# Reordering the first stage of a perceiver block: loads, first key products and two groups of queries

## The reference

```python
x = x + xattn(layernorm(x), context)   # 16 heads of 64; this is the layer that the change touches
x = x + gla(layernorm(x))              # gated linear attention, 4 heads
x = x + moe(layernorm(x))              # 8 experts, top 2, then layernorm

# xattn
q = tanh(x @ Wq);  k, v = split(context @ Wkv)
k = tanh(concat(null_key, k));  v = concat(null_value, v)
out = softmax(q k^T / 8) @ v           # over 1024 keys and the null key
return out @ Wout + bout
```

## Time and profile before

| | us |
|---|---|
| median of 3 runs | 219.04 (218.93 to 219.86) |
| profiled execution | 215.93 |
| its span, first to last instruction | 214.1 |
| TensorE busy | 194.7 (91%) |
| VectorE busy | 147.1 (69%) |
| ScalarE busy | 119.2 (56%) |
| GpSimd busy | 39.2 (18%) |
| mean granted TensorE clock | 0.992 |

### The profile page before, as it was taken

How to read it: one execution, slowest core, us unless ns; L and a number is a source line. 1 busy time by engine, 2 the same in 40 slices (tenths; PEclk the granted TensorE clock), 3 DMA queues, 4 the chain that set the end, 5 groups by cost and what they waited for, 6 DMA issues and landing times.

```text
span 214.1 us, 4143 instructions
## 1 busy us (share of the span) xinstructions
PE 194.7 (91%) x1621; PEld 146.2 (68%) x1621; DVE 147.1 (69%) x265; ACT 119.2 (56%) x218; POOL 39.2 (18%) x40
## 2 busy tenths in 40 slices
PE   6794879799999999999999999969888899999992
PEld 1692778688889898878889877946565334635560
DVE  3459798689888899998888869833892747134303
ACT  3197588588888888887888864102612113231300
POOL 4139202204022031220220800020501400000001
PEclk9999699999999999999999999999999999999999
DMA  5896559971103011010000596899999500000000
GB/s 170 283 388 171 134 164 369 367 205 54 49 3 98 3 49 52 0 49 3 0 5 0 193 384 211 288 385 378 377 377 377 175 0 0 3 0 0 5 0 26
DMA packets 22853, 31.02 MB, mean 145 GB/s; under 512 B 1953, under 2 KB 18866, under 8 KB 22834
## 3 DMA queue, kind: packets, MB, share of 16 engines
q1 hardware_dynamic: 22834, 30.76, 43.0%
HBM read 29.57 MB, written 0.13 MB: 139 GB/s over the span
## 4 chain that ended last, share of the span: by engine, by line
PE 45%; issue 22%; DVE 11%; DMA 8%; SPq 5%; ACT 5%; POOL 3%; POOLq 0%; DVEq 0%
PE ps L1001 30%; PE ps L1035 5%; DMA stage_t<-in_ctxT 4%; DMA w_k_stage<-in_Wkv 3%; SPq L433 3%; DVE keys L723 3%; PE ps L1075 2%; PE ps L1089 2%; DVE qx L835 1%; ACT keys L569 1%; DVE mixT L733 1%; POOL ctxT_l L477 1%; DVE att L862 1%; SPq L426 1%; PE ps L1152 1%
## 5 line engine op out<-in xcount | busy, mean ns | idle before, releaser
L723 DVE SCALAR_TENSOR_TENSOR keys<-ps,keys 64x512 f16<-64x512 f32 x64 | 44.1, 689 | 7.1 <-ACT keys L569 5.7
L1001 PE MATMUL ps<-ctxT_h,w_k_h 128*128 128x256 f32 x128 | 39.7, 310 | 3.1 <-POOL ctxT_l L477 1.6
L569 ACT ACTIVATE keys<-ps 64x512 f16<-64x512 f32 x64 | 37.8, 591 | 1.8
L1001 PE MATMUL ps<-ctxT_l,w_k_h 128*128 128x256 f32 x128 | 36.9, 288 | 0.0
L1001 PE MATMUL ps<-ctxT_h,w_k_l 128*128 128x256 f32 x128 | 36.7, 287 | 0.0
L1001 PEld LDWEIGHTS ps<-ctxT_h,w_k_h 128*128 128x128 f32 x128 | 25.0, 195 | 4.8 <-issue 2.4
L565 ACT ACTIVATE ps<-ps 128x512 f32<-128x512 f32 x32 | 18.6, 582 | 16.1 <-PE ps L1001 16.1
L689 DVE TENSOR_TENSOR ex_l<-ps,ex_h 128x512 fp32r<-128x512 f32 x32 | 22.1, 691 | 7.0 <-ACT ps L599 6.5
L1001 PE MATMUL ps<-ex_h,ctx_h 128*128 128x512 f32 x64 | 25.7, 401 | 0.0
L1001 PE MATMUL ps<-ex_l,ctx_h 128*128 128x512 f32 x64 | 25.3, 395 | 0.0
L1001 PEld LDWEIGHTS ps<-ctxT_l,w_k_h 128*128 128x128 f32 x128 | 25.2, 197 | 0.0
(11 more groups left out here) (173 smaller groups left out, 258.0 us busy)
## 6 DMA issues: line engine op xcount, KB each, us to landing
w<-in_fc1T SPq DMA_DIRECT2D x8, 1024.0 KB, 12.3
w<-in_fc SPq DMA_DIRECT2D x8, 1024.0 KB, 11.9
stage_t<-in_ctxT SPq DMA_DIRECT2D x8, 256.0 KB, 4.7
stage_n<-in_ctx SPq DMA_DIRECT2D x8, 256.0 KB, 4.1
w_k_stage<-in_Wkv SPq DMA_DIRECT2D x4, 256.0 KB, 5.4
mixT<-in_Wq SPq DMA_DIRECT2D x2, 512.0 KB, 6.3
q_two<-q_split SPq DMA_DIRECT2D x8, 128.0 KB, 4.4
w_v<-in_Wkv SPq DMA_DIRECT2D x1, 1024.0 KB, 5.3
```

The costliest lines, as they stand in the source:

```text
L569: nc.scalar.activation(keys[rows, u % 2, PK * i:PK * (i + 1), r], full[rows].rearrange("p (j n) -> p j n", j=PK), ACT.Copy, scale=UNIT).th ...
L723: V.scalar_tensor_tensor(out=keys[other, u % 2, PK * i:PK * (i + 1), r], in0=ps[mine, K_BANK + kp % 2].rearrange("p (j n) -> p j n", j=PK) ...
L1001: last = MM(dst, lhs[i], rhs[j], start=start and m == 0, stop=stop and m == len(parts) - 1)
```

## The change

SP's list is reordered: ctxT 0 first, then x, Wk 1, the identity, and the queries' weights and the rest of Wk by turns; the copies of the queries come ahead of the constants and the small loads. Wk 0 is loaded by ScalarE's own queue. TensorE makes key products 0 and 1 part by part as their operands become ready (`first_keys`), with the transposes in between, then the queries in two groups with keys 2 and 3 between and behind them; product 3 is done ahead of step 0 instead of in it. ScalarE and VectorE follow: VectorE makes the high part of context piece 0 and of Wk 2 and 3. GpSimd's memset of the sums moves to its beginning. In the steps one line changes: the high part of ctxT n+2 is made in step 4n + 1 instead of 4n + 3, in all pieces. The warm-up goes from 8 and 2 products to 7.

```diff
@@ SP
+            load_ctxT(0)
             sp.dma_start(x0[:], a["x"]).then_inc(ld_x, 16)
+            load_wk(1)
             sp.dma_start(const[:, 0:C_STRICT], a["const"][:, 0:C_STRICT]).then_inc(ld_eye, 16)
-            load_wk(0)
-            load_ctxT(0)
...
-            load_wk(1)
+            load_wq(0)
+            load_wk(2)
+            load_wq(1)
+            load_wk(3)
             sp.dma_start(null_k[:], a["null_k"]).then_inc(ld_null, 16)
             sp.dma_start(null_v[:], a["null_v"]).then_inc(ld_null_v, 16)
-            load_wk(2)
-            load_wk(3)
             load_ctx(0)
             load_ctxT(1)
             load_ctx(1)
...
+            spread_queries(0)
+            spread_queries(1)
             sp.dma_start(const[:, C_STRICT:], a["const"][:, C_STRICT:]).then_inc(ld_const, 16)
...
             sp.dma_start(b1[:], a["b1"]).then_inc(ld_small, 16)
...
-            spread_queries(0)
-            spread_queries(1)
@@ GpSimd
             nc.gpsimd.memset(minus_half[:], -0.5).then_inc(half_ready, 1)
+            nc.gpsimd.memset(ex_sum[:], 0.0).then_inc(zero_ready, 1)
...
-                    nc.gpsimd.memset(ex_sum[:], 0.0).then_inc(zero_ready, 1)
@@ ScalarE
+            act.dma_start(w_k_piece(w_k_stage, 0), w_k_source(0)).then_inc(ld_wk[0], 16)
             split_wk(0)
-            act.wait_ge(ld_ctxT[0], 16)
-            copy(ctxT_h[:, 0], stage_t[:, 0], first_high)
             split_wk(1)
+            keys_tanh(0)
+            keys_tanh(1)
+            queries_tanh(0)
             act.wait_ge(ld_null, 16)
             nc.scalar.activation(null_kt[:], null_k[:], ACT.Tanh).then_inc(nk_tanh, 1)
...
             keys_tanh(2)
+            queries_tanh(1)
+            null_exp(0)
+            keys_tanh(3)
@@ VectorE
+            dve.wait_ge(ld_ctxT[0], 16)
+            V.tensor_copy(ctxT_h[:, 0], stage_t[:, 0]).then_inc(first_high, 1)
+            dve.wait_ge(first_high, 1)
+            low_part(ctxT_l[:, 0], stage_t[:, 0], ctxT_h[:, 0]).then_inc(first_ready, 1)
+            low_wk(0)
...
-            split_wk(1)
+            high_wk(2)
+            low_keys(0)
+            high_wk(3)
             split_queries(0)
+            low_keys(1)
             high_ctxT(1)
-            low_keys(0)
+            low_keys(2)
             split_queries(1)
-            low_keys(1)
             high_ctx(0)
+            low_keys(3)
...
-                if t == KT - 1 and g == G - 1 and n + 2 < B * NC:
+                if t == KT - 1 and g == 0 and n + 2 < B * NC:
                     high_ctxT(n + 2)
@@ TensorE
+            def first_keys(kp, between=None):
...
+                pe.wait_ge(first_high, 1)
+                pe.wait_ge(wk_high, kp + 1)
+                products(w_k_h, ctxT_h, True, False)
+                pe.wait_ge(first_ready, 1)
+                products(w_k_h, ctxT_l, False, False)
+                if between:
+                    between()
+                pe.wait_ge(wk_ready[kp], 1)
+                products(w_k_l, ctxT_h, False, True).then_inc(k_psum, 1)
...
+            warm(7, 7)
+            first_keys(0)
+            first_keys(1, first_transposes)
+            queries(0)
             project_keys(2)
+            queries(1)
+            null_scores(0)
+            project_keys(3)
```

More of the change, by code:

```diff
@@ L263, in block_kernel @@
         wk_high = sem("wk_high")
+        wk_later = sem("wk_later")
         wk_ready = [sem(f"wk_ready{i}") for i in range(G * KT)]
@@ L365, in w_k_piece, with w_k_source @@
             return w[:, i // KT, :, (i % KT) * PK * P:(i % KT + 1) * PK * P]
+        def w_k_source(i):
+            return a["Wkv"][:, i * PK * P:(i + 1) * PK * P].rearrange("(c p) n -> p c n", p=P)
         block = whole.enter_context(nc.Block())
@@ L389, in load_wk, with load_wq @@
             def load_wk(i):
-                sp.dma_start(w_k_piece(w_k_stage, i),
-                             a["Wkv"][:, i * PK * P:(i + 1) * PK * P].rearrange("(c p) n -> p c n", p=P)).then_inc(ld_wk[i], 16)
+                sp.dma_start(w_k_piece(w_k_stage, i), w_k_source(i)).then_inc(ld_wk[i], 16)
+            def load_wq(half):
+                cols = slice(half * 512, (half + 1) * 512)
+                sp.dma_start(w_q[:, :, cols], chunked("Wq")[:, :, cols]).then_inc(ld_wq[half], 16)
             def chunked(name, p=P):
@@ L413, in _ @@
             load_ctx(1)
[L414 to L419, removed]
             def spread_queries(g):
@@ L430, in _ @@
             spread_queries(1)
+            sp.dma_start(const[:, C_STRICT:], a["const"][:, C_STRICT:]).then_inc(ld_const, 16)
+            sp.dma_start(bout[:], in_each_row("bout")).then_inc(ld_small, 16)
+            sp.dma_start(gamma[:], in_each_row("gamma")).then_inc(ld_small, 16)
+            sp.dma_start(beta[:], in_each_row("beta")).then_inc(ld_small, 16)
+            sp.dma_start(gnorm[:], in_each_row("gnorm")).then_inc(ld_small, 16)
+            sp.dma_start(b1[:], a["b1"]).then_inc(ld_small, 16)
             for e in range(E):
@@ L571, in keys_tanh, with queries_tanh, null_exp @@
                                          scale=UNIT).then_inc(k_high, 1)
+            def queries_tanh(g):
+                act.wait_ge(q_psum, g + 1)
+                nc.scalar.activation(qT[:, PG * g:PG * (g + 1)], ps[:, 1 + g].rearrange("p (j t) -> p j t", t=P),
+                                     ACT.Tanh).then_inc(q_tanh, 1)
+            def null_exp(g):
+                act.wait_ge(null_psum, g + 1)
+                nc.scalar.activation(null_ex[:, PG * g:PG * (g + 1)], ps[:, NULL_BANK[g]].rearrange("p (j t) -> p j t", t=P),
+                                     ACT.Exp, scale=DH ** -0.5).then_inc(null_ready, 1)
+            act.dma_start(w_k_piece(w_k_stage, 0), w_k_source(0)).then_inc(ld_wk[0], 16)
             split_wk(0)
-            act.wait_ge(ld_ctxT[0], 16)
-            copy(ctxT_h[:, 0], stage_t[:, 0], first_high)
             split_wk(1)
+            keys_tanh(0)
+            keys_tanh(1)
+            queries_tanh(0)
             act.wait_ge(ld_null, 16)
             nc.scalar.activation(null_kt[:], null_k[:], ACT.Tanh).then_inc(nk_tanh, 1)
[L579 to L589, removed]
             keys_tanh(2)
+            queries_tanh(1)
+            null_exp(0)
+            keys_tanh(3)
             for s in range(STEPS):
@@ L599, in _ @@
                 nc.scalar.activation(full, full, ACT.Exp, scale=SCORE_SCALE).then_inc(e_ready, 1)
-                if s + AHEAD < STEPS:
+                if s == 0:
+                    null_exp(1)
+                elif s + AHEAD < STEPS:
                     keys_tanh(s + AHEAD)
@@ L689, in low_part, with low_wk, high_wk @@
                 return V.tensor_tensor(dst, full, high.bitcast(F32), ALU.subtract)
-            def split_wk(i):
+            def low_wk(i):
                 dve.wait_ge(wk_high, i + 1)
                 low_part(w_k_piece(w_k_l, i), w_k_piece(w_k_stage, i), w_k_piece(w_k_h, i)).then_inc(wk_ready[i], 1)
+            def high_wk(i):
+                dve.wait_ge(ld_wk[i], 16)
+                V.tensor_copy(w_k_piece(w_k_h, i), w_k_piece(w_k_stage, i)).then_inc(wk_later, 1)
             def high_ctxT(n):
@@ L774, in _ @@
                     add_to_sum(s)
-                if s == 0:
-                    low_keys(2)
-                if s + AHEAD < STEPS:
+                if s >= 1 and s + AHEAD < STEPS:
                     low_keys(s + AHEAD)
@@ L1091, in output @@
                     last.then_inc(wo_psum, 1)
-            pe.wait_ge(warmer_ready, 1)
[L1095 to L1115, removed]
+            def first_keys(kp, between=None):
+                bank = ps[:, K_BANK + kp]
+                def products(w, x, first, last):
+                    for j in range(PK):
+                        cols = slice((PK * kp + j) * P, (PK * kp + j + 1) * P)
+                        for d in range(DC):
+                            ins = MM(bank[:, j * CK:(j + 1) * CK], w[:, 0, d, cols], x[:, 0, d, :],
+                                     start=first and j == 0 and d == 0, stop=last and j == PK - 1 and d == DC - 1,
+                                     skip_group_check=True)
+                    return ins
+                pe.wait_ge(first_high, 1)
[7 more added lines that the diff above has]
+                products(w_k_l, ctxT_h, False, True).then_inc(k_psum, 1)
@@ new lines, in first_transposes, with queries @@
+            def first_transposes():
+                pe.wait_ge(ld_eye, 16)
+                transpose_xn(0)
+            def queries(g):
+                pe.wait_ge(xnT_ready, 1)
+                pe.wait_ge(ld_wq[g], 16)
+                for j in range(PG * g, PG * (g + 1)):
+                    for c in range(DC):
+                        last = MM(ps[:, 1 + g, (j % PG) * P:(j % PG + 1) * P], w_q[:, c, j * P:(j + 1) * P],
+                                  xnT[:, c], start=c == 0, stop=c == DC - 1)
+                last.then_inc(q_psum, 1)
@@ L1116, in _, with null_scores @@
+            def null_scores(g):
```

(14 more changed lines are left out.)

9 lines of the change are left out of this document (2 added, 7 removed).

## The result

| | before | changed |
|---|---|---|
| median, us | 219.45 (4 runs, 218.93 to 220.02) | 225.24 (4 runs, 224.55 to 226.77) |
| profiled execution, us | 215.93 | 225.13 |
| its span, us | 214.1 | 223.3 |
| granted clock of TensorE | 0.992 | 0.961 |

The ratio is **1.042, 95% interval 1.038 to 1.046**: the change made the kernel slower. The two profiled executions are free of such a fall, so 9.2 us is the difference to be explained.

A forecast was written before the change was run, and what follows sets the result against it. Bound: a chain of waits through ctxT 2's load to product 8 at 41.01 us, then TensorE. Sum: +7.4 − 0.4 = +7.0 us, giving 222.9 us profiled and 226.0 us median, range 222.2 to 228.4.

The forecast's parts named there:

- The base: Whole kernel: the summed difference is added to the median, 219.04 us, with the profiled execution 3.11 us under it.
- the landing L of ctxT 2: Load of the third transposed context piece: issued at 30.5 us, lands at 18.0 + 18.71 + 3.08 = 39.8 us.
- The second group of queries: First stage: VectorE's split of queries 1 ends at 18.0 us, range 17.3 to 19.8; it was 20.43.
- The moved loads: SP's list: constants and five small loads now stand ahead of ctxT 2, 3.08 us; it lands at 39.8 us.
- The added wait: VectorE and TensorE wait for ctxT 2; the ninth key product, product 8, starts at 48.4 us, 7.4 later.
- The one gain: Change of batch: GpSimd's low part of a context piece is ready two steps earlier, −0.4 us, between 0 and −0.5.
- The wait of VectorE: End of step 1: VectorE is done at about 26 us and stands still nearly 14 us before casting ctxT 2.
- The start: First stage: the first twelve key products end at 7.1 us instead of 10.2, so 3 us are won.
- That ctxT 2 might not be held by the weights ahead of it: Load of ctxT 2, rival of no difference: it lands at 32.9 us, time 219.1 us; chance 5%.
- That the start's gain could arrive whole: First stage, rival of a faster kernel: ctxT 2 is there when VectorE comes at 26 us, 214.8 us; chance 4%.

The follow-up runs named there:

- e8: The changed kernel with the constants and five small loads issued ahead of the query copies again; median 221.48 us, ratio 1.028 to the kernel before.
- e7: The changed kernel with 50 warm-up products ahead of scores 4, keeping TensorE busy during the wait; median 226.09 us, ratio 1.051 to the kernel before.
- e4: The changed kernel with ctxT 2 loaded just ahead of the weights w_v and w_out; median 219.60 us, ratio 1.013 to the kernel before.
- e3: The changed kernel with ctxT 2 loaded right behind ctx 1, ahead of the query copies; median 219.25 us, ratio 1.012 to the kernel before.
- e6: The changed kernel with ctxT 2 loaded ahead of the query copies and ctxT 3 ahead of the weights; median 211.31 us, ratio 0.983 to the kernel before.
- e2: The kernel before with only the cast line changed, ctxT n+2 cast in step 4n+1; median 223.48 us, ratio 1.033 to the kernel before.
- e12: The kernel before with nine instead of four warm-up products at the start of the second layer; median 216.74 us, ratio 1.001 to the kernel before.
- e9: The kernel before with only two loads moved, ctxT 2 ahead of the query copies and ctxT 3 ahead of the weights; median 218.04 us, ratio 1.000.
- e10: The changed kernel with ctxT 2 and ctxT 3 loaded early and the cast back in step 4n+3; median 212.31 us, ratio 0.984 to the kernel before.
- e1: The changed kernel with the cast of ctxT n+2 back in step 4n+3; median 221.91 us, ratio 1.023 to the kernel before.
- run 17: A count, not a label: the unchanged kernel before, run 17 times; ten runs from 215.1 to 217.8 us, seven from 219.0 to 220.7.
- e11: The changed kernel itself, measured again beside the kernel before on one chip; median 226.70 us, ratio 1.049 to the kernel before.

## Why the prediction was wrong, and where it was right

The direction and the mechanism were right; the size was not. Against the profiled execution the sum said +7.0 us, with bounds of +3.2 and +9.4, and it was +9.2; as a ratio 1.032 was forecast and 1.042 measured. That 226.0 lies so near to 225.24 is luck: 3.1 us too much in the base and 2.2 too little in the sum cancel. The steps that failed are the base and, in the sum, the landing L of ctxT 2.

- **The base.** "I add the difference to the median", 3.11 us, was the first failed step. That difference is no constant of the measurement: the runs of the kernel before come in two groups some 3 us apart (last section), its median lay in the slower one and its profiled execution in the faster. The changed kernel's profiled execution, 225.13, lies at its median. The fair sum was 215.93 + 7.0 = 222.9 for the profiled execution, and 225.13 came.
- **"The second group of queries", 18.0 us.** It ended at 18.98. Wk 3 landed at 12.0, so that VectorE's cast of it came late, and the low part of queries 0 took 1.66 beside GpSimd: the split of queries 0 was done at 14.46 and not at 12.8. What follows it took 4.5 us, the undisturbed end of my bounds. Together 1.0 us.
- **"The moved loads", L = 39.8.** L was 41.46, and these 1.7 us are the largest part of the 2.2 that the sum lacked. Beside the 1.0 us above it is the landing itself, 10.17 instead of 9.33, 0.8 us. I had charged the moved loads to SP's list alone, 3.08; the list's part was right (from the split of the queries to the issue of ctxT 2 it is 12.3 us here and 9.0 in e8), but e8 shows 2.3 us more in the landing.
- **"The added wait", the mark at L + 8.6.** It was L + 9.15. The clock was low for step 4's first weighted sums as well, where I had counted them at full clock (step 4 took 4.37 us and not 3.9). The term as such (5.4 instead of 3.8, so 1.6) was confirmed by e7, at 1.9 us.
- **"The one gain", −0.4.** It was 0.6 from product 8 on, past my bound of 0.5. From 9.6 us at product 8 to 8.82 at the end of the stage it is 0.8, of which 0.2 lies in product 8 itself.
- **The final store**, +0.4, was in no term. With it the sum closes: 9.6 − 0.8 + 0.4 = 9.2.
- **The wait of VectorE, nearly 14 us.** 15.11. Step 1 was done at 26.37 as reckoned, the rest is the late landing.
- **The start (7.1 us).** Right: the first keys' tanh began at 7.19.
- **The rivals.** That ctxT 2 might not be held by the weights ahead of it falls by e4 (4.29 us without them). The fit in the Trainium skill, "DMA: Bandwidth & Descriptors", section "Anatomy of one DMA — SWDGE (gpsimd) path", from which 2.6 us was estimated for such a piece, agrees with the quickest of this kernel's (2.4 before, 2.6 changed) and not with the one that has 2 MB ahead (10.17). That the start's gain could arrive whole needed the load to be elsewhere, and e3 shows that even moving it is not enough: the next piece takes its place. With both moved it does arrive (e6, 5.3 us at the mark).

## What to carry to other kernels

Before an operation is moved earlier in an in-order engine, ask when its load lands, not when its buffer is free: the same cast idled VectorE for 1.9 us at the end of step 3, for 7.3 at the end of step 1 (e2), and for 15.1 there once the first stage was shorter and the load later. Everything queued behind it went along. A faster first stage shows in the time only if the first load that the steady part needs comes earlier too; here two lines in the list of issues turned a loss of 4.2% into a gain of 1.7%. And when one late load is moved, look at the next that stands behind large weights in the list.

## What the runs showed of the hardware

TensorE's clock falls after waits much shorter than those of this change, in some profiles and not in others. The second layer is the same in all variants but e12. Its first eight products, the projections of that layer's queries, took 2.00 us in e9 with a granted clock of 0.50 from 145 to 150 us (chain of e9):

```profile
143.34 2.00 PE ps L1154 x8
145.33 1.15 PE ps L1160 x2
```

The same place in e10, where the granted clock is 1.00:

```profile
139.98 1.09 PE ps L1200 x8
141.07 0.62 PE ps L1206 x2
```

In both profiles TensorE idles ahead of it 1.3 us for the layernorm and 0.5 for a copy. The profiles of e1 and e7 show the fall as well. From the mark to the end of the span it is 76.2 to 76.7 us in the three that have it, and 73.0 to 73.4 in all others, so it costs 3.2 or 3.3. The kernel before, run 17 times beside e11, came out in two groups of about that distance: ten runs from 215.1 to 217.8 us and seven from 219.0 to 220.7. That the fall makes the second group is an inference: no profile of the kernel before caught it.

```diff
-            warm(4, 7)
+            warm(9, 7)
             transpose_xn(1)
```

> The kernel before with nine instead of four warm-up products at the start of the second layer, where TensorE otherwise idles 1.3 us for the layernorm and 0.5 us for the transposed copy. The runs of the kernel before lie in two groups, near 216.5 and near 219.8 us, and in some profiles TensorE's clock falls right there and costs 3 us. Theory: the idle 1.3 us are its occasion, so most runs are now near 216.5 and their median falls by 2 to 3 us below that of the kernel before. If the fall has nothing to do with that gap, the runs still lie in two groups as before.

With five more warm-up products the 1.3 us shrink to 0.22 (the 0.5 stay), and twelve runs came out between 215.28 and 218.24 us, none at 219 or more; of seventeen runs of the kernel before beside them eight were above 219, three of these far above (280 to 381 us), which nothing here explains. The median of e12 is 216.74 against 217.87. The ratio, formed as in the first section, is 1.001: the warm-up does not speed up the faster group, it makes the slower one rarer. The median fell by 1.1 us and not by the 2 to 3 expected. That the gap is the occasion of the fall is likely by this, with twelve runs; why it comes in some runs only, and why e7, whose profile has it, was near 226 in all its runs, stays open.
